# Local attention on 32-partition tiles: another placement of keys, scores, turned probabilities and outputs in a fused eight-layer kernel

## The reference, cut to what matters

```python
qkv = (xw @ W_qkv).reshape(B * nw, WINDOW, 3, NUM_HEADS, HEAD_DIM)
q, k, v = (qkv[:, :, 0], qkv[:, :, 1], qkv[:, :, 2])
q = _layernorm(q, ln_gamma, ln_beta)
k = _layernorm(k, ln_gamma, ln_beta)
attn = jnp.einsum('bqhd,bkhd->bhqk', q * SCALE, k)
attn = jax.nn.softmax(attn, axis=-1)
out = jnp.einsum('bhqk,bkhd->bqhd', attn, v).reshape(B * nw, WINDOW, C)
out = out @ W_proj + b_proj
```

## Time and profile before

| | us |
|---|---|
| median of 3 runs (877.65 to 882.51) | 879.71 |
| the profiled execution | 876.92 |
| its span | 875.1 |
| TensorE, VectorE, ScalarE, GpSimd busy | 718.3, 682.1, 568.0, 399.3 |
| attention, first to last score maximum | 167.0 to 309.1 |

### The profile page before, as it was taken

The page is one execution under the profiler, slowest core; times in us unless marked ns, Lnnn a source line. Parts: engine busy times, 40 slices in busy tenths (PEclk is TensorE's granted clock), DMA queues, the critical chain, the costliest instruction groups (busy, mean ns, idle before and its releaser), DMA issues.

```text
span 875.1 us, 11013 instructions
## 1 busy us (share of the span) xinstructions
PE 718.3 (82%) x3306; PEld 463.8 (53%) x3306; DVE 682.1 (78%) x1609; ACT 568.0 (65%) x924; POOL 399.3 (46%) x435
## 2 busy tenths in 40 slices
PE   4778999689898979999769999977768667667787
PEld 3666776345454667777557777743222222222565
DVE  6666787698999648777768789977888878786784
ACT  5244666476684536665536677766789989788675
POOL 6627565545345105555319977743323334420330
PEclk9889999997998669999979999978899999999999
DMA  4200000001000000000001000000000000000001
GB/s 136 73 12 14 16 15 16 25 24 31 19 25 7 12 1 1 1 1 1 1 0 37 1 1 0 1 0 1 1 0 1 1 1 1 1 0 1 1 0 49
DMA packets 9610, 11.59 MB, mean 13 GB/s; under 512 B 720, under 2 KB 5712, under 8 KB 9552
## 3 DMA queue, kind: packets, MB, share of 16 engines
q1 hardware_dynamic: 9552, 10.89, 4.3%
HBM read 9.84 MB, written 1.05 MB: 12 GB/s over the span
## 4 chain that ended last, share of the span: by engine, by line
PE 37%; DVE 24%; ACT 16%; POOL 12%; issue 10%; DMA 0%; DVEq 0%; ACTq 0%; POOLq 0%
POOL rbuf L1034 3%; PE y_bank L733 3%; PE gate_banks L1265 2%; PE spread_bank L1288 2%; DVE B L1752 2%; PE gate_banks L733 2%; ACT B L1765 2%; DVE B L1247 2%; POOL WL L2175 2%; PE gate_banks L735 2%; PE gate_banks L734 2%; PE y_bank L735 2%; PE y_bank L734 2%; PE up_banks L733 2%; DVE XN L408 2%
## 5 line engine op out<-in xcount | busy, mean ns | idle before, releaser
L1034 POOL TENSOR_TENSOR rbuf<-B,rbuf 128x512 fp32r<-128x512 f32 x96 | 124.3, 1297 | 83.6 <-ACT rbuf L962 83.3
L996 DVE TENSOR_TENSOR B<-B,up_banks 128x512 f32<-128x512 f32 x68 | 46.5, 684 | 42.8 <-PE up_banks L735 26.2
L947 ACT ACTIVATE B<-gate_banks 128x512 f32<-128x512 f32 x68 | 40.5, 598 | 58.8 <-PE gate_banks L735 57.7
L499 POOL TENSOR_SCALAR small<-small 128x4 f32<-128x4 f32 x32 | 8.1, 252 | 145.3 <-DVE small L389 144.6
L962 ACT ACTIVATE rbuf<-B 128x512 fp32r<-128x512 f32 x100 | 62.5, 625 | 14.1 <-DVE B L1012 11.1
L1012 DVE TENSOR_TENSOR B<-B,spread_bank 128x512 f32<-128x512 f32 x96 | 64.7, 680 | 7.1 <-ACT B L951 3.9
L733 PE MATMUL gate_banks<-XH,WH 128*128 128x512 f32 x152 | 66.6, 438 | 0.8 <-ACT YT L1357 0.8
L1762 ACT ACTIVATE B<-B,VEC 128x1024 f32<-128x1024 f32 x48 | 55.4, 1154 | 14.4 <-DVE B L1757 14.4
L735 PE MATMUL gate_banks<-XH,WL 128*128 128x512 f32 x152 | 62.0, 408 | 0.0
L734 PE MATMUL gate_banks<-XL,WH 128*128 128x512 f32 x152 | 61.8, 407 | 0.0
L1247 POOL TENSOR_SCALAR B<-S,WR 128x128 f32<-128x128 f32 x64 | 39.2, 628 | 44.8 <-DVE S L1229 37.8
(11 more groups left out here) (348 smaller groups left out, 2257.2 us busy)
## 6 DMA issues: line engine op xcount, KB each, us to landing
STG<-in_w_split SPq DMA_DIRECT2D x27, 256.0 KB, 2.7
X<-in_x SPq DMA_DIRECT2D x4, 256.0 KB, 4.5
out<-X SPq DMA_DIRECT2D x4, 256.0 KB, 2.3
WR<-in_w_raw SPq DMA_DIRECT2D x1, 524.5 KB, 4.0
STG<-in_w_exact SPq DMA_DIRECT2D x2, 256.0 KB, 2.7
STG<-in_w_split SPq DMA_DIRECT2D x5, 64.0 KB, 1.9
STG<-in_w_split SPq DMA_DIRECT2D x1, 192.0 KB, 2.3
STG<-in_w_split SPq DMA_DIRECT2D x1, 128.0 KB, 2.1
```

The costliest lines, as they stand in the source:

```text
L1034: e_.tensor_tensor(lo, hidden(f, n), hi.bitcast(F32), ALU.subtract).then_inc(hl_ready, 1)
```

## The change

The 128 partitions hold 16 heads of 8, so 32 partitions hold 4. The masks now single out one head in each group of 4: `attn_keys` makes four copies of a whole chunk's keys (128x512, scale and bias of the norm folded in), two on ScalarE and two on GpSimd, once for each chunk, instead of 16 copies for each tile. A score unit is four matmuls of 32 partitions x 64 queries x 256 columns, for two windows `w` and two groups of heads `k`. Each `k` has its own bank, and both units use the same two banks (`SB2`), the columns from 256 on of these banks hold turned outputs. `weigh` now has the values stationary (18 columns) and the turned probabilities streaming (64 columns); four pairs of heads go to four column groups. Its result has heads on partitions, so ScalarE copies it (`copy_out`) and TensorE turns it back (`attn_turn_out`), four units later; `finish` runs once a unit, on all 128 partitions. The mean of squares lies with tokens on partitions (16 columns a matmul), root and reciprocal work on 128x128, ScalarE spreads the result over the heads (`attn_spread_act`) and TensorE turns it. The placing of V takes 2 instructions instead of 8. The split of the outputs for the projection moves from VectorE to GpSimd (`attn_project_pool`, same two operations).

The order changes too. TensorE's unit n is scores n+1, turn n, weigh n-1 (before: turn n-1, scores n+1, weigh n-2). ScalarE's is copy of n-1, exponential of n, output copy of n-2, then: at 0 the placing of V, at 1 and 2 the squares and copies of Q and K, at 3 root and V's copies, at 4 the spread and the copy of the old chunk's outputs, at 6 the projection's copy and the keys; hooks as before. GpSimd has keys at 5 and the split at 4. The turn of the old chunk's outputs at 3 waits for the new chunk's V copy. The tail's hook is at 7. Score unit 0 is issued in FFN0, between its down products of block 5 and block 6 of the last chunk, and the early steps of chunk 0 move (`EARLY_AT`).

```diff
         QN = [S0[:, 0:CH], S0[:, CH:2 * CH]]
-        KN = [S0[:, 2 * CH:3 * CH], S0[:, 3 * CH:4 * CH]]
         Zf = Z[:, :, :].rearrange("p a b -> p (a b)")
         AT = [Zf[:, 0:CH], Zf[:, CH:2 * CH]]
         qc, kc = Zf[:, 2 * CH:3 * CH], Zf[:, 3 * CH:4 * CH]
-        KM = [B[:, 4 * k_:4 * k_ + 4, :].rearrange("p a b -> p (a b)").rearrange("p (h t) -> p h t", h=NH)
-              for k_ in range(2)]
-        PRB = [buf[8], buf[9]]
-        PT = [buf[10], buf[11]]
+        KM = [B[:, 8:12, :], B[:, 4:8, :]]
+        PRB = [buf[0], buf[1]]
+        HALF = KG * WIN
+        TURN_W = HALF + WIN
+        PT = [S0[:, 2 * CH:3 * CH], buf[2]]
+        OT = [S0[:, 3 * CH + k * P:3 * CH + (k + 1) * P] for k in range(2)]
+        SBW = GG[:, :].rearrange("p (k x) -> p k x", k=2)
+        SB2 = SBW[:, :, 0:HALF]
+        LAG = 4
+
+        def out_cols(M):
+
+            k = max(0, M - (NU - LAG))
+            return slice(HALF + k * WIN, HALF + (k + 1) * WIN)
         WK = sb("WK", [P, 3, CH])
         sqq, sqk = WK[:, 0, :], WK[:, 1, :]
-        sdev, rstd = WK[0:GR, 2, :], WK[0:GR, 0, :]
+        sdev, rstd = WK[:, 2, 0:TL * GR], WK[:, 2, TL * GR:2 * TL * GR]
         A32w = WK[:, 1, :]
...
-        PREPARE_AT = {1: 0, 2: 1, 3: 2, 5: 3}
+        PREPARE_AT = {0: (0,), 1: (1,), 2: (3, 2), 4: (4,), 5: (5,)}
+        COPY_AT = {1: (0,), 2: (1,), 3: (2, 3)}
+        EARLY_AT = {0: (0,), 1: (1,), 2: (2,), 4: (4,), 5: (5,), 6: (3,)}
 
...
                 pe.wait_ge(centred, 2 * c + 2)
-                nc.tensor.matmul(R[0:GR, :], raw("mean_k"), sqk, start=True, stop=False)
-                nc.tensor.matmul(R[0:GR, :], raw("mean_q"), sqq, start=False, stop=True).then_inc(var_full, 1)
+                for j in range(TL):
+                    for sq, name, at_ in ((sqq, "mean_q", 0), (sqk, "mean_k", NH)):
+                        i = nc.tensor.matmul(R[:, j * GR + at_:j * GR + at_ + NH], sq[:, j * P:(j + 1) * P],
+                                             raw(name, at_, NH), start=True, stop=True)
+                i.then_inc(var_full, 1)
...
+            if step in (4, 5):
+                pe.wait_ge(rstd_wide, 2 * c + step - 3)
+                if step == 5:
+                    pe.wait_ge(qk_read, 2 * c + 1)
+                for j in range(TL):
+                    i = nc.tensor.matmul(R[:, j * P:(j + 1) * P], (sqq, QN[c % 2])[step - 4][:, j * P:(j + 1) * P],
+                                         ident, start=True, stop=True)
+                i.then_inc(rstd_full, 1)
...
+        def attn_spread_act(a, c):
+
+            a.wait_ge(rstd_qk, c + 1)
+            if c >= 2:
+                a.wait_ge(s_full, UN * (c - 1))
+            for dst, at_ in ((sqq, NH), (QN[c % 2], 0)):
+                nc.scalar.activation(dst.rearrange("p (t h d) -> p t h d", t=TL, d=HD),
+                                     bcast(rstd.rearrange("p (t h) -> p t h", t=TL)[:, :, at_:at_ + NH].unsqueeze(3),
+                                           [P, TL, NH, HD]), ACT.Copy).then_inc(rstd_wide, 1)
...
+        def attn_keys(eng, c):
+
+            if c >= NC:
                 return
...
+            eng.wait_ge(qk_read, 2 * c + 1)
+            if c >= 2:
+                eng.wait_ge(s_full, UN * (c - 1))
+            elif c == 1:
+                eng.wait_ge(yt_ready, count(2, 0))
+            for j in ((0, 1) if eng is nc.scalar else (2, 3)):
+                dst = KM[c % 2][:, j, :]
                 if eng is nc.scalar:
-                    i = eng.activation(dst, src, ACT.Copy, scale=raw("head_mask", h, 1))
-                else:
-                    i = eng.tensor_scalar(dst, src, raw("head_mask", h, 1), None, ALU.mult)
-            i.then_inc(done, 1)
+                    i = eng.activation(dst, kc, ACT.Identity, scale=key_g[:, j:j + 1], bias=key_b[:, j:j + 1])
+                else:
+                    i = eng.tensor_scalar(dst, kc, key_g[:, j:j + 1], key_b[:, j:j + 1], ALU.mult, ALU.add)
+            i.then_inc(keys_act if eng is nc.scalar else keys_pool, 1)
+
+        def attn_turn_out(pe, M):
+            pe.wait_ge(o_copied, M + 1)
+            for k in range(2):
+                rows = slice(64 * k, 64 * k + 64)
+                i = nc.tensor.transpose(SBW[:, k, out_cols(M)], OT[M % 2][rows, :], ident[rows, rows])
+            i.then_inc(o_turned, 1)
+
+        def attn_scores(pe, N):
+            if N >= NU:
+                return
+            u, c, i_ = N % 2, N // UN, N % UN // 2
+            if N % UN == 0:
+                pe.wait_ge(keys_act, c + 1)
+                pe.wait_ge(keys_pool, c + 1)
+                pe.wait_ge(qk_ready, c + 1)
+            if N:
+                pe.wait_ge(s_read, N)
+            else:
+                pe.wait_ge(act_done, NC * FFN0.blocks)
+            if N > LAG:
+                pe.wait_ge(o_read, N - LAG)
+            if N >= LAG:
+                attn_turn_out(pe, N - LAG)
+            for w in range(2):
+                tok = slice(i_ * P + w * WIN, i_ * P + (w + 1) * WIN)
+                for k in range(2):
+                    rows = slice(32 * (2 * u + k), 32 * (2 * u + k) + 32)
+                    i = nc.tensor.matmul(SB2[w * WIN:(w + 1) * WIN, k, :], QN[c % 2][rows, tok],
+                                         KM[c % 2][rows, :, tok], start=True, stop=True)
+            i.then_inc(s_full, 1)
 
         def attn_pe(pe, c, hook):
...
                 pe.wait_ge(pt_ready, N + 1)
                 if N % (UN // 2) == 0:
                     pe.wait_ge(v_placed, N // (UN // 2) + 1)
-                if u == 0 and tile:
-                    pe.wait_ge(o_read, tile)
-                for q in range(4):
-                    pr = 4 * u + q
-                    i = nc.tensor.matmul(SP[:, pr * 36:(pr + 1) * 36], PT[u][:, q * P:(q + 1) * P],
-                                         VB[:, tile % TL, pr, :, :, :].rearrange("p a b d -> p (a b d)"),
-                                         start=True, stop=True)
+                if N:
+                    pe.wait_ge(o_copied, N)
+                for w in range(2):
+                    for q in range(4):
+                        at_ = q * P + w * WIN
+                        i = nc.tensor.matmul(SP[32 * q:32 * q + 2 * (HD + 1), u * P + w * WIN:u * P + (w + 1) * WIN],
+                                             VB[:, tile % TL, w, 4 * u + q, :, :].rearrange("p h d -> p (h d)"),
+                                             PT[u][:, at_:at_ + WIN], start=True, stop=True)
                 i.then_inc(o_full, 1)
 
             nxt = c + 1 < NC
...
             for n in range(UN):
                 N = c * UN + n
-                if n == 6 and nxt:
-                    attn_prepare_pe(pe, c + 1, 4)
+                if n == UN - 1 and c:
+                    hook(-1)
+                attn_scores(pe, N + 1)
+                turn(N)
                 if N:
-                    turn(N - 1)
-                scores(N + 1)
-                if N >= 2:
-                    weigh(N - 2)
+                    weigh(N - 1)
                 if n == 0:
                     attn_values_pe(pe, c, 1)
                     if c == 0:
                         hook(-1)
+                if nxt:
+                    for step in PREPARE_AT.get(n, ()):
+                        attn_prepare_pe(pe, c + 1, step)
                 if n == 3 and c:
                     attn_turn_pe(pe, c - 1)
-                if n == 4 and c:
+                if n == 5 and c:
                     attn_project_pe(pe, c - 1)
-                attn_hooks(n, c, hook, 4)
-                if n in PREPARE_AT and nxt:
-                    attn_prepare_pe(pe, c + 1, PREPARE_AT[n])
+                attn_hooks(n, hook)
                 if n == 7 and nxt:
                     attn_values_pe(pe, c + 1, 0)
...
-        def attn_hooks(n, c, hook, tail_at):
-
-            if n == tail_at and c:
-                hook(-1)
-            for pos in {0: (0,), 1: (4,), 2: (1, 5), 3: (11, 2, 6), 4: (3, 7), 5: (8,), 6: (9,)}.get(n, ()):
+        def attn_hooks(n, hook):
+
+            for pos in {0: (0,), 1: (4,), 2: (1, 5), 3: (2, 6), 4: (7,), 5: (3, 8), 6: (9,)}.get(n, ()):
                 hook(pos)
...
+                O = SBW[:, :, out_cols(M)].rearrange("p k (q m) -> p k q m", q=2)[:, :, :, 0:2 * (HD + 1)]
+                rec_ = orec[:, HU * u:HU * u + HU]
+                chain(nc.vector.reciprocal(rec_.rearrange("p (k q h) -> p k q h", k=2, q=2), O[:, :, :, HD::HD + 1]))
+                for k in range(2):
+                    i = nc.vector.tensor_tensor(
+                        AT[c_ % 2][:, i_ * P + u * WIN + k * 32:i_ * P + u * WIN + (k + 1) * 32]
+                        .rearrange("p (q h d) -> p q h d", h=2, d=HD),
+                        O[:, k, :, :].rearrange("p q (h d) -> p q h d", h=2)[:, :, :, 0:HD],
+                        bcast(rec_[:, 4 * k:4 * k + 4].rearrange("p (q h) -> p q h", h=2).unsqueeze(3), [P, 2, 2, HD]),
+                        ALU.mult)
                 i.then_inc(o_read, 1)
...
```

(61 more changed lines are left out.)

208 lines of the change are left out of this document (95 added, 113 removed).

## The result

The changed kernel takes 869.75 us (median of 4 runs, 869.11 to 871.40) against 879.66 in the same session (877.65 to 882.51): ratio 0.9874, 95% interval 0.9842 to 0.9906. It is faster, by 9.9 us; forecast were 24.7. The direction held, and so did the wide range for 8 in 10 (827 to 885); the size did not, and 869.75 lies outside the 840 to 865 that the prediction gave to its own mechanism. The profiled execution has a span of 868.3 us.

The account below looks back on a forecast made before the run. VectorE, over 90% busy in the first three attention windows, was taken to set the pace. From 876.9, 21 (chunks), 2.4 (start) and 1 (reciprocal) came off: 852.5, put at 855 for the runs' median; 8-in-10 range 827 to 885.

Parts of the forecast that it names:

- its own mechanism: Attention stage: engines no longer overlap across units, so each unit's slowest engine adds up; 840 to 865 us, chance 0.50.
- rival B: Attention scores: row tiles do not overlap, 1.0 to 1.4 us each; 13 to 25 us back, about 872; chance 0.13.
- the 0.4 us more: Attention units on TensorE: a drain of 0.3 us at changes of tiling mode would add 0.4 us a unit.
- Rival D: Attention stage: engines overlap after all, chunk falls to TensorE's own 24.2 us, gain 50, total 825; chance 0.15.
- full-clock sum of 29.9: Attention chunk at full clock: the slowest engine's time in each of eight units, summed to 29.9 us.
- Rival E: Attention units: the one bank serialises everything, 4.65 us a unit, no gain, about 878; chance 0.10.
- with 15% of the time there: Attention stage: TensorE at half clock for 15% of the time, giving 31.6 us a chunk.
- The prediction's formula: Attention chunk: 1/((1-s)/29.9 + s/46) for share s at half clock; 31.6 us, 21 us gained over four chunks.
- less since gaps shrink: Attention stage: the half-clock share, 0.26 in the windows before, would fall as gaps shrink; taken as 15%.
- the prediction's own sign of being wrong: Attention stage: the forecast would be wrong if the clock stayed low for over half of the stage.
- rival C: Attention stage: TensorE stays at half clock, 46 us a chunk, total 911; decides from share 0.54; chance 0.12.
- The start: Start of attention: down products 1.6 us later, first exponential at about 166 instead of 168.4, 2.4 us gained.

Follow-up runs that it names:

- g_keys: Changed kernel with GpSimd's first-chunk keys made earlier, inside the feed-forward network's last chunk before its weight pieces; 859.0 us.
- x_keys2: Changed kernel with GpSimd's two keys of the first chunk made twice; 867.2 us.
- x_keys5: Changed kernel with GpSimd's two keys of the first chunk made five times; 878.5 us.
- a_scores0: Changed kernel with score unit 0 issued at the start of attention again, behind the last two down products; 859.7 us.
- gc_best: g_keys with the residual hook of the experts' last chunk moved from unit 0 to unit 1 on VectorE and TensorE; 867.6 us.
- ge_notable: g_keys with a plain scaled copy in place of the root, so no table loads in units 3 and 4; 864.3 us.
- the control: The changed kernel once more, unaltered, with six further runs; 866.3 us.

## Why the prediction was right or wrong

**Right.** VectorE's work (83.7 us in the windows, forecast 89) and its reciprocal (0.94 us, forecast 0.85). TensorE's new pieces are each within 0.2 us of their price: rival B (row tiles one after another, 1.0 to 1.4 us) is refuted by scores at 0.59. The Trainium skill (TensorEngine Tiling (Array Packing), Key Properties) states that a change of tiling mode drains the engine. The unit with its four changes took 1.73 us here, so the 0.4 us more that the prediction held possible did not come. Rival D is refuted by chunk 2, 31.0 us against its 24.2 and the forecast's full-clock sum of 29.9. Rival E's 4.65 a unit, 37.2 a chunk, is refuted by the same row. GpSimd's keys cost 0.76 us each in chunk 0 and 1.02 in the other three, forecast 0.7. The end of the stage took 10.3 us from last subtract (299.7) to the projection's copy (310.0), in the forecast range of 10.3 to 12.

**Right in sum, wrong inside.** In chunk 2 the reduce-to-reduce times are 3.0, 3.7, 3.3, 4.3, 2.9, 7.8, 2.9, 3.0. Unit 5 takes twice the forecast 3.6: the turned spread comes late, because ScalarE makes it behind its table load, exponential and copy of unit 4. I had priced that as a unit of its own slowest engine, not as a wait that carries over; units 2 to 4 were cheaper by about as much (10.5 us, forecast 14.0). That the two cancel is luck.

**The step that failed: "with 15% of the time there".** The prediction's formula mixes the two clocks by the share of time at half clock. Put the measured share in, 1/(0.50/29.9 + 0.50/46) = 36.2 us a chunk; measured are 139.1/31 x 8 = 35.9. For g_keys it gives 34.2 (34.0), for x_keys2 34.5 (34.5), for x_keys5 37.2 (36.7).

Elsewhere it is less close: 35.6 for a_scores0 (34.6, clock 0.76) and 36.2 for gc_best (35.0, clock 0.75). By chunks of the changed kernel it is off by up to 2.3 us either way, too short in chunk 0 (42.5, measured 44.4) and too long in the last seven units (32.6, measured 30.3). So it carries the size of the loss, not its tenths.

With 15% it gave 31.6. I argued "less since gaps shrink" from the earlier trace rows; the share was 0.50. Even the share of the kernel before, 0.28, would have given 33.1 us a chunk and 14 us of gain instead of 21. The 0.50 stands at the prediction's own sign of being wrong (a low clock for over half of the stage) and near rival C's turning point, which its formula puts at 0.53 (the prediction says 0.54). So C's mechanism came half true, though the cause was not the small tiles alone: the same tiles ran at 0.82 in g_keys. At half clock the preparation grows most where all wait for it: the variance's 16 records take 3.43 us instead of 1.86, and unit 3 of chunk 0 7.8 us instead of 4.3.

**The start: gain forecast, loss measured.** The prediction knew that scores 0 would wait for GpSimd's keys and that two down products stood behind, and priced it at 1.6 us. The wait was 3.81, and scores at half clock 1.1. The first exponential came at 165.72 (168.41 before), but the network before had ended 4 us sooner in this profile (VectorE's last product with the router's weights began at 152.9 instead of 156.9). Of these 4 us 3.1 were there at 132, ahead of the first changed instruction of TensorE; they go mostly with the clock, which was at half from 35.8 to 49.4 before and full from 41.5 to 48.4 after. So the step lost 1.3 us instead of gaining 2.4, and 3.1 us of the profiled gain come from ahead of the changed work. And the exponential was the wrong mark: VectorE stood 8.7 us in the residual hook, and the second reduce came at 171.1 (171.7 before).

**What the miss consists of.** g_keys removes the wait for the keys and stands at 859.0, 4 us from the forecast. That this is so near is partly luck: its stage still takes 131.6 us where 122 were forecast, and its first reduce comes at 155.3 where the forecast had the scores done at 162.3. In the profiles it is 6.0 us ahead of the changed kernel at the second reduce (165.2 against 171.1; 0.7 of it older than the edit) and 11.3 at the end of chunk 0 (192.3 against 203.6). So about 5 us are the wait and another 5 the half clock of that chunk.

Whether TensorE's standing brings the low clock is not shown. In chunk 0 the kernels with the wait of 3.8 us or more had 32 to 41 us at half clock, but x_keys2 17; those without it had 9 to 29 (g_keys 14, a_scores0 28, ge_notable 29); and x_keys5's 10.29 us of wait brought 39 where 3.81 had brought 38. The wait makes a long half clock likelier in these profiles, and no more can be said; why the clock took just this course stays open.

Finally, of 12.2 us that the projection's last copy was ahead of before (310.0, 322.2), 8.8 were left after the next network's second block, which ran at half clock until 321.4, and 6.8 from the third network's start to the end of the kernel. The first of these losses did not recur in the control's profile (12.8 us ahead at the copy, 12.5 at that block), the second did (11.0 at the end). The prediction had carried the stage's gain to the end whole.

## What to carry to other kernels

When work is hoisted into an earlier stage's queue, list each of its inputs and when the slowest producer gets to it; a wait there is paid by everything queued behind, and if TensorE stands meanwhile, perhaps again as half clock. Hoist the producers first: one call moved forward on GpSimd was worth 7 to 11 us here, about as much as the whole change had brought. When a change takes work off the bounding engine, forecast TensorE's time at both clocks and let the share at half clock run from what it was (0.28 here) up to a little over one half (0.36 to 0.56 in the variants that keep the root), instead of assuming that it falls.

## What the hardware showed that I had not expected

Two row groups by two column halves (32 x 64 tiles) stream at once: eight records of 256 columns in 0.59 us, nearly as cheap as the four-fold column tiles of the earlier trace rows, half of whose 0.99 us would be 0.50. The Trainium skill (TensorE: Matmul & The Clock Gate, What's actually happening) says that for modelling, the penalty of the clock's ramp is below 1% of a typical kernel's span. Here the clock went to and fro, and the stage alone took 139.1 us where 31 units of the full-clock sum are 116, 2.7% of the span; without the 8.6 us by which unit 0 of chunk 0 exceeds its forecast 3.3, 1.7%. The course of the clock repeated almost to the tenth of a microsecond in two executions of one kernel in different sessions (chunks 44.4, 33.3, 31.0 and 44.4, 33.4, 31.1), and yet with 1.6 us more of waiting it was 39.1 instead of 44.4. A step of 1 or 2 us can thus not be judged by the time alone there. And with the table loads gone from ScalarE the mean clock of the stage was 0.67 instead of 0.75, and the time was where it had been.
